# The second layer of the last 24 steps as a 2 x 2 block product in seven products

## What is computed

```
def step(carry, xw_t):                 # 64 times, one after the other
    a = xw_t + prev_h @ Wh             # [32, 256] @ [256, 1024]
    i, f, o = sigmoid(a[:, :3 * Hd] in three parts); g = tanh(a[:, 3 * Hd:])
    next_c = f * prev_c + i * g
    next_h = o * tanh(next_c)

h = concatenate([h, -h]); h = relu(s0 * (h @ K0)) * 2      # first layer
h = relu(s1 * (h @ K1)) * 2                                # second layer, 1024 x 1024
return x + s2 * (h @ K2)                                   # third layer
```

## Time and profile before

| | |
|---|---|
| time, median of 3 runs | 277.18 us (277.06 to 278.49) |
| the profiled execution | span 276.0 us; its page gives no other time of its own |
| PE busy | 272.2 us, 99% |
| DVE, ACT, POOL busy | 203.5, 158.0, 2.2 us |
| last matmuls of step 63 | begin at 227.62 us |
| last matmul of all | ends at about 273.4 us |

### The profile page before, as it was taken

How to read it: one execution, slowest core, us unless ns; L and a number is a source line. 1 busy time by engine, 2 the same in 40 slices (tenths; PEclk the granted TensorE clock), 3 DMA queues, 4 the chain that set the end, 5 groups by cost and what they waited for, 6 DMA issues and landing times.

```text
span 276.0 us, 8792 instructions
## 1 busy us (share of the span) xinstructions
PE 272.2 (99%) x3616; PEld 224.0 (81%) x3616; DVE 203.5 (74%) x751; ACT 158.0 (57%) x482; POOL 2.2 (1%) x10
## 2 busy tenths in 40 slices
PE   8999999999999999999999999999999999999996
PEld 5887888888999998999999999999999996444443
DVE  3778888878888888888888888888887876532213
ACT  5689787878566656655555566555665554411100
POOL 0200000000000000000000000000000000000000
DMA  6970000000000000000000000000000000010002
GB/s 221 362 298 1 4 2 0 2 4 2 2 2 0 5 21 21 2 2 4 21 23 2 1 21 21 2 2 23 22 3 0 21 23 2 0 38 2 0 0 76
DMA packets 5191, 8.72 MB, mean 32 GB/s; under 512 B 672, under 2 KB 3488, under 8 KB 5024
## 3 DMA queue, kind: packets, MB, share of 16 engines
q1 hardware_dynamic: 4864, 7.64, 7.8%
q10 hardware_dynamic: 288, 0.52, 0.5%
HBM read 6.07 MB, written 2.10 MB: 30 GB/s over the span
## 4 chain that ended last, share of the span: by engine, by line
PE 97%; DMA 1%; DVE 0%; DVEq 0%; issue 0%
PE WK L465 50%; PE WK L448 14%; PE G L427 11%; PE ACC L481 10%; PE G L418 9%; DMA x<-in_x 1%; PE G L448 1%; PE ACC L448 1%; PE G L481 0%; DVE xs L715 0%; DVE x L662 0%; DVEq L237 0%
## 5 line engine op out<-in xcount | busy, mean ns | idle before, releaser
L465 PE MATMUL WK<-h,k 128*128 128x256 f16 (+1 forms) x992 | 124.2, 276 | 0.0
L465 PEld LDWEIGHTS WK<-h,k 128*128 128x128 fp8e5 x992 | 94.2, 98 | 13.4
L609 ACT ACTIVATE tT<-aT 128x128 f32<-128x128 f32 x126 | 39.0, 310 | 56.4 <-DVE aT L759 55.2
L655 DVE SCALAR_TENSOR_TENSOR h<-WK,h 128x256 f16<-128x256 f32 (+1 forms) x105 | 42.6, 439 | 24.7 <-ACT h L574 24.7
L759 DVE TENSOR_REDUCE aT<-G 128x128 f32<-128x256 f32 x128 | 48.1, 417 | 7.7 <-PE G L427 6.1
L574 ACT ACTIVATE h<-WK 128x256 f16<-128x256 f32 (+1 forms) x104 | 36.3, 387 | 28.8 <-PE WK L465 28.8
L556 ACT ACTIVATE G<-xw 128x256 f32<-128x256 f32 x126 | 46.6, 370 | 0.0
L448 PE MATMUL WK<-xs,wxs 128*128 128x512 f32 x168 | 42.5, 400 | 0.0
L427 PE MATMUL G<-h,w 128*128 128x64 f16 x1008 | 39.5, 192 | 0.0
L418 PEld LDWEIGHTS G<-h,w 128*128 128x128 f16 x1008 | 32.9, 96 | 5.8 <-DVE h L776 4.4
L448 PEld LDWEIGHTS WK<-xs,wxs 128*128 128x128 f32 x168 | 30.4, 188 | 5.9
(11 more groups left out here) (66 smaller groups left out, 132.8 us busy)
## 6 DMA issues: line engine op xcount, KB each, us to landing
x<-in_x SPq DMA_DIRECT2D x3, 512.0 KB, 7.8
out_y<-x SPq DMA_DIRECT2D x12, 128.0 KB, 1.8
xw<-in_wh SPq DMA_DIRECT2D x4, 256.0 KB, 4.8
k<-in_k SPq DMA_DIRECT2D x1, 1024.0 KB, 9.6
x<-in_x ACTq DMA_DIRECT2D x2, 256.0 KB, 3.8
xw<-in_wx SPq DMA_DIRECT2D x4, 128.0 KB, 3.9
xw<-in_wx SPq DMA_DIRECT2D x2, 256.0 KB, 5.1
k<-in_k SPq DMA_DIRECT2D x1, 512.0 KB, 6.9
```

Source lines behind the costliest of these rows:

```text
L465: ins = eng.matmul(layer_src(tile), w, rhs, start=a == 0, stop=last)
L609: eng.activation(tT[:, B * j0:B * j1], aT[:, j0:j1].rearrange("p j b -> p (j b)"), ACT.Tanh, scale=half_gain0 if t == 0 else half_gain).th ...
L655: eng.scalar_tensor_tensor(layer_dst(tile, 1), layer_src(tile), 0.0, layer_dst(tile, 0), ALU.max, ALU.subtract).then_inc(lo_made[tile[0]])
```

## The change

**Chunks.** The last 24 steps are now two chunks of 12 steps (384 columns, `NW`): number 5 (`N1`) and number 6 (`N2`).

**Seven products.** For these two chunks the second layer is written as a product of 2 x 2 blocks: weights A (blocks of 512 x 512: a11, a12, a21, a22) times activations B (rows: two halves of the 1024 inputs, k 0 to 3 and 4 to 7; columns: chunk N1 and chunk N2). Seven block products p1 to p7 replace eight. A product is 4 tiles (m) of 8 matmuls of 384 columns. p2 is summed on top of p1 in the same bank (after p1 has been copied out), p6 on top of p5, p7 on top of p6 in the same way.

**Sums of weights.** Three of the products need sums of weight blocks (`mix`, fp8). POOL makes them in 32 pieces of 256 columns (`mix_part`), one each step from step 10 on, released by the end of the step's low part of h (`hl_made`).

**Sums of activations.** B's column N2 is needed as b22 and four combinations `tq[0]` to `tq[3]`, each 4 blocks of 128 x 384 and split in a high and a low part. For k = 0 to 3, when tiles k and 4+k of the first layer are summed: ACT `n2_relu`, `n2_hi`; DVE `n2_terms` (four instructions); ACT `term_hi(0, k)` and `term_hi(1, k)`. The low parts (`term_lo`) of 0 and 3 and the fourth combination (`term4`) are POOL's, those of 1 and 2 DVE's, in a row at the end.

**Sums of results.** The products are combined on DVE and POOL with fp32 copies that ACT takes out of PSUM (`p1_copy`, `p3_copy`, `p5_copy`), then split by `c_split` (ACT) and `c_rest` (DVE).

**Order.** `fill` allows 2.3 instead of 2.44 us of layer work in a step from 16 on. A step's list may now hold one low part of a layer and one `y_add` where it held at least two low parts. The gate banks G hold tiles in the tail. The output of N2 is sent before that of N1. x is laid out without the cut in four.

```
-CHUNKS = ((0, 8), (8, 8), (16, 8), (24, 8), (32, 8), (40, 8), (48, 16))
+CHUNKS = ((0, 8), (8, 8), (16, 8), (24, 8), (32, 8), (40, 12), (52, 12))
+MIX_STEP, MIXES = 10, 32
...
-    return 3.4 if t < 0 else 1.8 if t < 1 else 2.3 if t < 9 else 2.2 if t < 16 else 2.44
+    return 3.4 if t < 0 else 1.8 if t < 1 else 2.3 if t < 9 else 2.2 if t < 16 else 2.3
...
+    order = [((0, N2, m + 4 * half), a) for m in range(4) for half in (0, 1) for a in range(4)] + left
+    order += [(("p3", m), 2 * k + part) for k in range(4) for m in range(4) for part in (0, 1)]
+    order += products(5, 0, 1) + first_outs + products(6, 0, 1) + products(7, 0, 1) + products(4, 0, 1) + products(5, 2, 3)
+    order += outs(N2, 0, 1) + products(6, 2, 3) + outs(N2, 4, 5) + products(7, 2, 3) + outs(N1, 4, 5) + products(4, 2, 3)
+    return order + outs(N2, 2, 3, 6, 7) + outs(N1, 6, 7)
...
+        factors = {1: (a11, b1[:, 0:4]), 2: (a12, b1[:, 4:8]), 3: (mix[:, 3], b22), 4: (a22, tq[:, 3]),
+                   5: (mix[:, 0], tq[:, 0]), 6: (mix[:, 1], tq[:, 1]), 7: (mix[:, 2], tq[:, 2])}
+        out_parts = {N1: (11, c11, 21, c21), N2: (12, c12, 22, c22)}
...
+            for k in range(4):
+                n2_relu(k)
+                n2_hi(k)
+                term_hi(0, k)
+                term_hi(1, k)
             for tile in act_plan[T]:
-                layer_hi(tile)
+                empty(tile)
+            for i, k in ((3, 0), (3, 1), (2, 0), (2, 1), (2, 2), (2, 3), (3, 2), (3, 3)):
+                term_hi(i, k)
+            for m in range(4):
+                p3_copy(m)
+            for ms in ((0, 1), (2, 3)):
+                for m in ms:
+                    p5_copy(m)
+                for q in (12, 22, 21):
+                    for m in ms:
+                        c_split(q, m)
...
+            def n2_terms(k):
+                b, d = layer_src((0, N2, k)), layer_src((0, N2, 4 + k))
+                e.wait_ge(r12_made, k + 1)
+                e.wait_ge(r1_made, k + 1)
...
+                eng.scalar_tensor_tensor(t1f[:, k % 2], b, 0.0, r1[:, k], ALU.max, ALU.subtract).then_inc(t_made[0])
+                e.wait_ge(hi22, k + 1)
+                e.wait_ge(t_made[0], k + 1)
+                eng.scalar_tensor_tensor(t23[:, 0, k], d, 0.0, t1f[:, k % 2], ALU.max, ALU.subtract).then_inc(t_made[1])
+                eng.scalar_tensor_tensor(t23[:, 1, k], d, 0.0, r12[:, k % 2], ALU.max, ALU.subtract).then_inc(t_made[2])
+                eng.scalar_tensor_tensor(b22[:, k, 1], d, 0.0, b22[:, k, 0], ALU.max, ALU.subtract).then_inc(lo22)
...
+            for n in range(MIXES):
+                mix_part(n)
+            for k in range(4):
+                term_lo(0, k)
+                if k >= 1:
+                    term_lo(3, k - 1)
+                term4(k)
+            term_lo(3, 3)
```

More of the change, by code:

```diff
@@ L107, in tile_order @@
     order.append((("x", 3, 7), 6))
-    for c in range(NC):
+    for c in range(N1):
         for m in range(8):
@@ L189, in make_plan @@
                 continue
+            if tile[0] in ("x", 0, 1, "p2"):
+                free.append((bank[tile], tile))
             if tile[0] != "o":
-                free.append((bank[tile], tile))
                 finished.append((tile, spent))
             elif tile[2] == 7:
[L194 to L200, removed]
+                finished += [(("y", tile[1], mo), spent) for mo in range(2)]
+        if 0 <= t and any(tile[0] == "x" for tile, _ in pe[t]):
             pe[t].sort(key=lambda p: p[0][0] == "x")
@@ L228, in make_plan @@
         todo = [x for x in todo if x not in now] + late
-        if t == T - 1:
-            dve[t] += todo
-            emptied.update(todo)
+    dve[T] = todo
+    rest = []
+    if piece < len(order):
+        order[piece] = (order[piece][0], left)
+    for tile, n in order[piece:]:
+        for _ in range(n):
+            rest.append((tile, done.get(tile, 0)))
+            done[tile] = done.get(tile, 0) + 1
+    free += [(NWK + 2, ("g", 0)), (NWK + 3, ("g", 1))]
+    at, empty_at = 0.0, {old: 0.0 for _, old in free}
+    for tile, a in tail_order(rest):
+        free.sort(key=lambda b: empty_at[b[1]])
+        if tile[0] == "o" and tile[1] == N2 and a == 0 and tile[2] == 0:
+            for mo in range(2):
+                bank["y", mo], before["y", mo] = free.pop(0)
+        place(tile)
+        pe[T].append((tile, a))
+        at += cost(tile)
+        if a + 1 == matmuls(tile) and tile[0] in (0, 1, "p2", "p3", "p4", "p7"):
+            free.append((bank[tile], tile))
+            empty_at[tile] = at + 1.2
+            if tile[0] == 0 and tile[1] == N2:
+                empty_at[tile] = 2.35 * (tile[2] % 4) + (1.5 if tile[2] < 4 else 3.3)
+    finished = [tile for tile, a in pe[T] if a + 1 == matmuls(tile)]
+    act[T] = [x for x in finished if x[0] in (1, "p1", "p2") or x[0] == 0 and x[1] == N1]
+    for x in finished:
+        if x[0] in (1, "p2") or x[0] == 0 and x[1] == N1:
+            dve[T + 1].append(x)
+        if x[0] == "o" and x[1] < N1 and x[2] == 7:
+            dve[T + 1] += [("y", x[1], mo) for mo in range(2)]
     return pe, act, dve, bank, before
@@ L478, in out_matmul @@
                     e.wait_ge(y_made[mo], c)
[L479 to L482, removed]
+                ins = eng.matmul(ACC[mo][:, 0:width(tile)], w2[:, k, 128 * mo:128 * mo + 128],
+                                 h2[:, k % NH2, part, 0:width(tile)], start=k == 0 and part == 0, stop=k == 7 and part == 1)
@@ L793, in _ @@
                 empty(tile)
+            for k in range(4):
+                n2_terms(k)
+            for tile in dve_plan[T + 1]:
+                empty(tile)
+            for i in (1, 2):
+                for k in range(4):
+                    term_lo(i, k)
+            for ms in ((0, 1), (2, 3)):
+                for q, c_sum_of in ((12, c12_sum), (22, c22_sum), (21, c21_sum)):
+                    for m in ms:
+                        c_sum_of(m)
+                    for m in ms:
+                        c_rest(q, m)
+            for c in (N2, N1):
+                for mo in range(2):
+                    y_add(c, mo)
         @block.gpsimd
```

384 lines of the change are left out of this document (286 added, 98 removed).

## The result

| | before | the change |
|---|---|---|
| time, median (lowest to highest) | 277.46 us (277.06 to 278.49, 4 runs) | 281.84 us (281.59 to 282.44, 4 runs) |
| span of the profiled execution | 276.0 us | 279.9 us |

The ratio is 1.0155, with a 95% interval of 1.0129 to 1.0182: slower by more than 0.5%. The forecast was 280.7 us, 3.5 us above the kernel before; measured are 4.4 us between the medians and 3.9 between the spans.

The account below looks back on a forecast made before the run. PE's queue was taken to bound the kernel. The terms -5.1 + 1.6 + 2.8 + 3.6 + 0.6 = +3.5 us gave 280.7 us, with an 8-in-10 range of 277.0 to 283.5; the forecast had a chance of 0.54.

Parts of the forecast that it names:

- What bounds the kernel: Whole kernel: PE is busy 272.2 of 276.0 us, so a removed matmul saves its time and a PE wait costs its time.
- Columns, -5.1: Second layer of the last 24 steps: 224 matmuls of 384 columns, 36.5 us, replace 41.6 us of matmuls.
- Uneven steps, +1.6: Steps with short lists, such as 45 and 51, and long ones behind them: PE waits for h; bounds 0.6 to 2.5.
- The weight sums, nothing: POOL's pieces in the steps: a window of 1.5 us hides each if it costs between 0.37 and 0.74 us.
- The four blocks, +2.8: Tail: 2.10 us a block makes PE wait for banks (0.1, 0.8) and for the copy of p1's last tile (1.85).
- Combination 0 on POOL, +3.6: Tail, inside p5: PE waits for POOL's late low part; 2.4 to 4.3 if POOL and DVE exclude each other, 0.5 otherwise.
- P: Cost of one POOL instruction of 384 elements and two inputs in the tail: taken as 0.95 us, bounds 0.55 and 1.11.
- The rest, +0.6: Tail: products behind p5 wait some 0.2 for queued copies; two y_add behind the last sums add 0.4 at the end.
- POOL and DVE side by side: Rival, tail: the engines do not exclude each other, the wait is 0.5 instead of 3.6, total 277.6 us; chance 0.23.
- The copy of p1 in time: Rival, tail: DVE's part runs beside ACT's, the copy's wait falls from 1.85 to 0.3, total 275.3 us; chance 0.11.
- The weight sums did fit: Answers the rival that pieces of 1.7 us delay the cell update 0.2 in 32 steps, total 287.1 us; chance 0.06.
- PE's clock: Rival, tail: the clock falls behind long waits, 3 us of work at half speed, +3, total 283.7 us; chance 0.06.

Follow-up runs that it names:

- p7 above: The fastest version that computes everything (276.25 us), without 28 of the 32 matmuls of product p7: 272.32 us, ratio 0.9801.
- the version with more equal steps: The changed kernel with POOL and ACT reordered, N1's last sums finished bank by bank, and planner numbers giving more equal lists: 276.25 us, ratio 0.9955.
- The experiment: The changed kernel with POOL's 32 weight-sum pieces released in the middle of the cell update, not behind the low part of h: 291.92 us, ratio 1.0528.
- the first experiment: The changed kernel with the copy of p1's last tile moved on ACT ahead of the fourth block's two term_hi: 280.39 us, ratio 1.0096.
- the run that held DVE back: The changed kernel with DVE's eight term_lo waiting until POOL has made the fourth low part of combination 0: 283.13 us, a single run.
- two reorderings of those queues: The changed kernel with p1's last copy earlier on ACT and POOL making all low parts of combination 0 first: 278.23 us, ratio 1.0021.

## Why the prediction was right, point by point

Each term of the sum was paid where it was said to be, but about half of the loss in the steps has another cause than the one given, and the largest term lies outside its own bounds. That 280.7 came so near is in part luck: the largest term was 1.4 us too dear, and the others together 1.9 too cheap (steps 0.6, blocks 0.9, the rest 0.6, less 0.2 at the start).

**What bounds the kernel** held: PE's queue, so that a saved matmul counts in full (p7 above) and each wait too.

**Columns, -5.1.** Held. In the chain of the changed kernel 24 matmuls of 384 columns take 3.90 us, 0.163 each.

**Uneven steps, +1.6.** Measured 2.2, inside the bounds of 0.6 and 2.5. PE's timeline ahead of three of the four steps named:

```profile
165.85 0.56 PE L485 MATMUL G<-h,w 128*128 128x32 f16 x16 [0.39 <-DVE h L1023]
...
185.56 0.57 PE L485 MATMUL G<-h,w 128*128 128x32 f16 x16 [0.28 <-DVE h L1023]
...
209.25 0.57 PE L485 MATMUL G<-h,w 128*128 128x32 f16 x16 [0.35 <-DVE h L1023]
```

These stand ahead of steps 46, 52 and 59; ahead of 47 PE lost under 0.1 us. The price of a short list was wrong: steps 45 and 51, with 15 and 16 layer matmuls, both lasted 3.06 us, so the shortest step is 3.06 and not 2.85. The walk took 0.24 us from the first L427 to the first sum, the time of half its matmuls in the queue, where the earlier trace rows have 224.63 - 224.20 = 0.43, and no step of either kernel has less. These two steps lose 1.0 us. Nearly all the rest stands in steps in which DVE makes two or three low parts (L846) ahead of the first sum: the sum begins 0.6 to 1.1 us behind the first L494 in place of 0.43 (steps 41, 56, 58 and 60), and 1.0 us is lost there, 0.5 of it in step 58, which I had named. That the order of DVE's work does it is read from the trace and was not tried; that PE's lists alone don't, the version with more equal steps shows.

**The weight sums, nothing.** Held: 0.64 us a piece, inside 0.37 to 0.74, ended before the next instruction that reads SBUF alone. The experiment shows what hides them: moved by half a step they cost 10 us.

**The four blocks, +2.8.** Measured 3.3 from the starts: 0.3 and 0.9 for the two banks, 2.1 for the copy of p1 (1.85 was said). A block takes 2.19 us where I had 2.10; nearly all of the difference is one hand-over, between DVE's own first two instructions, which took 0.10 and not 0.03. The two between engines took 0.03 to 0.04, as said. That the copy was the cause, and not the length of the chain, the first experiment shows. Another 0.4 before the first tile, a wait for the low part of h, I had not priced.

**Combination 0 on POOL, +3.6.** The mechanism was right, the size not: 2.2, under the 2.4 to 4.3 that taking turns was to give. P was 0.92 and 1.02, the 0.95 taken. Two things were off in what DVE adds. The four of combination 1 did not go first: POOL and DVE began at 238.51 and 238.53. And a turn of DVE costs POOL 0.31 us, not DVE's whole 0.48: the six instructions took 7.03 us with five turns between them and 5.46 with DVE held back. A pair takes 1.24 where 0.91 and 0.47 would be 1.38, so part of each instruction runs beside the other's. Also, the copy of p1 came 0.25 later than in my walk, but that shifts both sides.

L1019 lasts as long as POOL's instruction beside it, and L888 takes 1.24 us a pair with POOL's; without that, the wait was to be 0.5, and it was 0.5 in the run that held DVE back. The rule of the Trainium skill that I weighed there (SBUF — State Buffer, "SBUF: two separate sides": an exclusive lock on shared ports, the other engine blocked until the end) is borne out by this in its kind. Its size is not: the 0.31 us that a turn of DVE costs POOL is less than DVE's instruction. The price of a two-input fp32 instruction that I worked out from the Trainium skill (GPSIMD Engine Reference, "Elementwise — side-by-side cycle accounting"), an estimate of 0.84, was 0.07 to 0.18 too low.

**The rest, +0.6.** 0.6 for the products behind p5 where 0.2 was said, and 0.6 at the end where it was 0.4. The 0.5 us by which the difference of the medians exceeds that of the spans (4.4 and 3.9) was not predicted. Of it, 0.3 is the choice of the execution: other executions of the kernel before took 1.8 us more than their span, so the profiled one, with 276.0, stands for about 277.8 and not for the median of 277.46. The other 0.2 is time outside the span, 2.0 us in the change.

**The rivals.** POOL and DVE side by side fell by 1.24 against 0.92. The copy of p1 in time fell, by a wait of 1.9; the version in which it does come in time won 1.45, near the 1.55 that the rival had for the copy. The weight sums did fit. PE's clock reads full (1.00) in every stretch of the changed kernel's trace, and 384 columns kept their 0.163 behind waits of 2 us. But it can fall there. In the traced execution of the first experiment PE stood for 2.0 us before the same place in p5; from 246 to 248 us its granted clock was 0.50, the level of 1.2 GHz, and the 24 matmuls from 245.14 on took 5.58 us where they cost 3.90. The page's clock row, then PE's timeline:

```profile
PEclk9999999999999999999999999999999999979999
...
244.81 0.48 PE L550 MATMUL WK<-xw,mix 128*128 128x384 f16 x2 [1.96 <-POOL xw L1084]
245.14 2.54 PE L550 MATMUL G<-xw,mix 128*128 128x384 f16 x8
247.47 3.41 PE L581 MATMUL ACC<-h,k 128*128 128x384 f16 x16
250.72 1.46 PE L550 MATMUL WK<-xw,mix 128*128 128x384 f16 x8
```

That execution took 1.6 us more than the median of its five. One of the run with the weight sums moved looks alike by its time (293.31 us, mean clock 0.992), and has no trace. Of the 14 executions of versions that keep POOL's wait of 0.5 us or more inside p5 these are the only two under a mean clock of 0.998; the 38 of versions without it have none. So the rival named something real, at about half the price it had; in the four executions of the change it did not come up, and what decides it is not shown.

## What to carry to other kernels

A scheme that saves an eighth of the matmuls of a stretch puts its sums on the other engines, and there its gain is decided by the order of their queues: here 5.1 us of matmuls were bought with 9.0 us, nearly all of them waits, 4.3 from one copy behind sixteen instructions and one low part behind another engine's late one, and two reorderings of those queues won 3.6 us. So for each new instruction, ask what stands ahead of it in its own queue and what that waits for; an instruction whose operand is late belongs behind all those that are needed earlier and have theirs.
Give POOL a place in which DVE reads an operand from PSUM, not SBUF alone: POOL's 0.92 us beside `n2_terms` and its 0.64 us behind the low part of h cost neither engine anything. Where they do meet, price a turn of each, and read the shortest step of a chain from start to start, not from the costs of its parts.

## What was not expected of the hardware

A DVE instruction with a single SBUF operand (L1019, 64 fp32 elements, `tensor_scalar`) was held as long as POOL's fp8 instruction beside it ran, 0.65 us for 0.19; I had expected that of instructions with two. And in the tail the two engines took strict turns, neither starved: eight DVE instructions in 9.89 us with 7 of POOL's between them, whose starts lie 1.2 to 1.3 apart. A pair was 0.14 us cheaper than the two alone, so a part of each ran beside the other; which part, the records don't say.
